# Graph attention and a routed expert layer on one core: order of the first projections, who scales the last chunk, and in which step a tile's residual, norm and routing are done

## The reference, cut to what matters

```python
def gnn(x, adj, W, b_W, a_vec, b_a):           # N = 2048 nodes, D = 128
    h = x @ W.T + b_W
    e = (h @ a1)[:, None] + (h @ a2)[None, :] + b_a[0]
    e = where(e > 0, e, 0.2 * e)
    scores = where(adj > 0, e, -9e15)
    return softmax(scores, axis=1) @ h

def ffn(x, Wr, br, W1, b1, W2, b2):            # 64 experts, 128 -> 256 -> 128
    logits = x @ Wr + br
    topk_logits, topk_idx = top_k(logits, 2)
    gates = softmax(topk_logits)
    # out = sum over the two chosen experts of gate * (relu(x W1 + b1) W2 + b2)

x = x + gnn(layernorm(x), adj, ...)
x = x + ffn(layernorm(x), ...)
```

## Time and profile before

| what | us |
|---|---|
| median of 3 runs (293.38 to 293.85) | 293.51 |
| the profiled execution's own time | 295.59 |
| its span, from the first to the last instruction | 293.8 |
| busy: PE, DVE, ACT, POOL | 229.1, 220.0, 173.5, 167.5 |
| mean granted TensorE clock, as a share of full speed | 0.895 |

### The profile page before, as it was taken

One profiled execution on the slowest core, in us unless ns is written; L12 is line 12 of the kernel. 1 busy time (PEld: TensorE's weight loads), 2 busy tenths in 40 slices (PEclk: granted clock), 3 DMA queues, 4 the chain that ended last, 5 costly groups with the idle time before them and its releaser, 6 DMA issues.

```text
span 293.8 us, 6191 instructions
## 1 busy us (share of the span) xinstructions
PE 229.1 (78%) x1849; PEld 219.6 (75%) x1849; DVE 220.0 (75%) x643; ACT 173.5 (59%) x386; POOL 167.5 (57%) x193
## 2 busy tenths in 40 slices
PE   1491698596959779586997463999999999999840
PEld 1271698596959769585996352999999999999840
DVE  4858959949599986999997550588888666666554
ACT  2754665755765496567653602688786777777410
POOL 5840104325175982978886565344688888876500
PEclk9998599988897979899799655799999999999995
DMA  6992730644847386150298012212226830100057
GB/s 165 223 190 48 101 62 1 122 130 134 224 74 186 120 214 182 45 232 31 64 425 331 32 48 59 72 58 74 66 81 220 275 138 31 38 27 31 26 186 254
DMA packets 11120, 36.88 MB, mean 126 GB/s; under 512 B 2257, under 2 KB 2833, under 8 KB 10321
## 3 DMA queue, kind: packets, MB, share of 16 engines
q0 software_dynamic: 5232, 14.98, 22.5%
q1 hardware_dynamic: 5424, 21.11, 21.1%
q10 hardware_dynamic: 432, 0.40, 0.6%
HBM read 39.36 MB, written 5.51 MB: 153 GB/s over the span
## 4 chain that ended last, share of the span: by engine, by line
PE 44%; DVE 28%; POOL 9%; DMA 7%; issue 6%; ACT 4%; SPq 1%; POOLq 0%; DVEq 0%; ACTq 0%
PE bank L1089 16%; PE bank L1101 15%; DVE arena L697 7%; PE bank L986 6%; DVE arena L691 6%; POOL rstd L403 3%; POOL table L420 3%; POOL nm L405 2%; DMA arena<-result 2%; DMA xs<-in_x 2%; DVE arena L682 2%; DVE xs L703 1%; PE bank L938 1%; PE bank L1078 1%; ACT rows_in L546 1%
## 5 line engine op out<-in xcount | busy, mean ns | idle before, releaser
L986 PE MATMUL bank<-arena 128*128 128x130 f32 x512 | 64.8, 287 | 3.0 <-ACT arena L540 3.0
L986 PEld LDWEIGHTS bank<-arena 128*128 128x128 f32 x512 | 63.5, 204 | 3.9 <-issue 3.9
L1089 PE MATMUL bank<-arena 128*128 x384 | 61.1, 284 | 0.1
L1101 PE MATMUL bank<-w2s,arena 128*128 x384 | 59.2, 277 | 0.2 <-issue 0.2
L972 PE MATMUL bank<-ident,arena 128*128 128x128 f32 x256 | 39.0, 317 | 22.4 <-DVE arena L697 22.3
L420 POOL DMA_INDIRECT table<-rows_in,pos x32 | 46.8, 1464 | 15.9 <-issue 7.8
L972 PEld LDWEIGHTS bank<-ident,arena 128*128 128x128 f32 x256 | 34.9, 165 | 24.0 <-DVE arena L697 24.0
L1089 PEld LDWEIGHTS bank<-arena 128*128 128x128 f32 x384 | 52.1, 197 | 0.6 <-issue 0.3
L1101 PEld LDWEIGHTS bank<-w2s,arena 128*128 128x128 f32 x384 | 51.1, 194 | 0.6 <-issue 0.6
L868 DVE SCALAR_TENSOR_TENSOR arena<-bank,arena 128x128 f32 x96 | 33.6, 350 | 22.5 <-PE bank L1101 15.2
L599 ACT ACTIVATE arena<-bank,arena 128x128 f32<-128x128 f32 x96 | 35.2, 366 | 19.3 <-PE bank L1089 14.4
(11 more groups left out here) (191 smaller groups left out, 270.9 us busy)
## 6 DMA issues: line engine op xcount, KB each, us to landing
arena<-in_adj POOLq DMA_DIRECT2D x16, 512.0 KB, 6.5
w2s<-in_w SPq DMA_DIRECT2D x8, 768.0 KB
arena<-in_w SPq DMA_DIRECT2D x6, 1024.0 KB
arena<-in_w SPq DMA_DIRECT2D x4, 512.0 KB
w2s<-in_w SPq DMA_DIRECT2D x4, 512.0 KB
xs<-in_x SPq DMA_DIRECT2D x4, 256.0 KB, 6.4
arena<-result SPq DMA_DIRECT2D x2, 512.0 KB, 4.3
arena<-result SPq DMA_DIRECT2D x4, 256.0 KB, 6.2
```

The lines of the kernel that those rows point to most:

```text
L986: ins = pe.matmul(OB[t % 2][:, 0:D + 2], pt_r[:, t % 2, j, :], h[:, j, :], start=(j == 0), stop=(j == T - 1))
L1089: ins = pe.matmul(hp(p, b), w1u[:, p % UW, P * b:P * b + P], xT_all[:, bass.ds(column, P)], start=True, stop=True)
L1101: ins = pe.matmul(yp(p), hT[:, p % UH, b, :], w2s[:, bass.ds(u, 1), b, :].rearrange("p e d -> p (e d)"), start=(b == 0), stop=(b == HB - 1))
```

## The change

It has eight edits.

1. TensorE's start: after the first two chunks' transposes come piece 0 of the score row, the transposes of chunk 2, piece 1, the projections of chunk 0, the transposes of chunk 3, pieces 2 and 3 back to back, and behind them the projections of chunks 1 to 3.
2. VectorE scales chunk 3 (with a semaphore of its own, `s_norm3`); ScalarE scales chunks 0 to 2 only. GpSimd issues the adjacency loads 2 and 3 behind the last `nm2`. VectorE does `penalty(0)` right after its first copy, and `scores(0)` after two of the eight `h_evac`; six follow it. `s8` is made in two pieces.
3. VectorE's loop: `residual(s-3)` stands ahead of `leaky(s-1)`, where `residual(s-2)` stood behind it; `residual(13)` follows the loop.
4. ScalarE's norms come in even steps from 4 on, ahead of evac: norm(s-4), norm(s-3). GpSimd's `rstd_of` follows, one step later and behind that step's load; tile 8's scatter goes from step 14 to 15.
5. Routing on TensorE and ScalarE stands inside a tile: `route_a(q)` at the head of attend(LAST[q]+2), `route_b(q)` in its middle; ScalarE's `route_a` in the middle of that tile's evac. Group 4 had this form before.
6. `top2` and `place`: two operations over k become one of twice the size (L733, L750); the position is written to its integer tile in one step.
7. The row numbers (`ids`) are written to `rows_out` once, by GpSimd at the start, no longer by VectorE in each `place` (L757).
8. The last sums with b2 go in four groups of four tiles, where there were six groups.

```diff
-    PLACED = [..., (1, 7, 14), (2, 8, 14), (2, 9, 15)]
+    PLACED = [..., (1, 7, 14), (2, 8, 15), (2, 9, 15)]
...
 # gpsimd
+            pool.tensor_copy(rows_out[:, :, :, ID_COL], ids[:, :, :])
...
-                if c < 3:
-                    load(c + 1)
+                if c == 0:
+                    load(1)
+            load(2)
+            load(3)
...
             for s in range(T):
-                if s >= 3 and s % 2 == 1:
-                    rstd_of(s // 2 - 1)
                 if s + 5 < T:
                     load(s + 5)
+                if s >= 4 and s % 2 == 0:
+                    rstd_of(s // 2 - 2)
...
 # scalar
-            scale(3)
...
             def evac(t):
                 for b in range(4):
+                    for q in range(NG):
+                        if b == 2 and t == LAST[q] + 2:
+                            route_a(q)
...
-                for q in range(INLOOP):
-                    if s == LAST[q] + 3:
-                        route_a(q)
+                if s >= 4 and s % 2 == 0:
+                    norm(s - 4)
+                    norm(s - 3)
                 if s >= 1:
                     evac(s - 1)
-                if s >= 3 and s % 2 == 1:
-                    norm(s - 3)
-                    norm(s - 2)
...
+            norm(T - 4)
+            norm(T - 3)
             evac(T - 1)
             norm(T - 2)
-            route_a(4)
             route_b(4)
...
 # vector
-                for k in range(TOPK):
-                    ins = dve.tensor_tensor(hot[:, k, kept(q), :], ..., ALU.is_equal)
-                link(ins)
+                link(dve.tensor_tensor(hot[:, :, kept(q), :], ..., ALU.is_equal))
...
-                link(dve.scalar_tensor_tensor(posf[:, :, 0:n], ...))
                 dve.wait_ge(s_gate, q + 1)
-                dve.tensor_copy(rows_out[:, rows, :, ID_COL], ids[:, rows, :])
                 dve.tensor_copy(rows_out[:, rows, :, GATE_COL], ...)
-                dve.tensor_copy(pos[:, rows, :]..., posf[:, :, 0:n]).then_inc(s_pos, 1)
+                dve.scalar_tensor_tensor(pos[:, rows, :]..., idxf..., float(STRIDE), rank...).then_inc(s_pos, 1)
...
             xT_evac(0)
-            xT_evac(1)
             penalty(0)
+            dve.wait_ge(s_nm, 4)
+            for t in range(12, T):
+                ins = dve.tensor_scalar(xh[:, t, :], xs[:, t, :], rstd[:, t:t + 1], nm2[:, t:t + 1], ALU.mult, ALU.add)
+            ins.then_inc(s_norm3, 1)
+            xT_evac(1)
             xT_evac(2)
+            penalty(1)
             dve.wait_ge(s_was, 1)
             h_evac(0)
             h_evac(1)
-            penalty(1)
-            for c in range(2, 6):
-                h_evac(c)
+            dve.wait_ge(s_hs, 2)
+            dve.tensor_scalar(s8[:, 0:4], h[:, 0:4, D], 1.0 - SLOPE, None, ALU.mult).then_inc(s_s8, 1)
             scores(0)
-            h_evac(6)
-            h_evac(7)
+            for c in range(2, 8):
+                h_evac(c)
...
+                if s >= 3:
+                    residual(s - 3)
                 leaky(s - 1)
-                if s >= 2:
-                    residual(s - 2)
...
+            residual(T - 3)
             leaky(T - 1)
             residual(T - 2)
...
 # tensor
             def attend(t):
                 if t >= 2:
                     pe.wait_ge(s_x1, t - 1)
-                if t == T - 1:
-                    route_a(4)
+                for q in range(NG):
+                    if t == LAST[q] + 2:
+                        route_a(q)
                 for j in range(T):
                     b = j // CB
-                    if t == T - 1 and j == T // 2:
-                        route_b(4)
+                    for q in range(NG):
+                        if j == T // 2 and t == LAST[q] + 2:
+                            route_b(q)
```

More of the change, by code:

```diff
@@ L451, in _ @@
             rstd_of(8)
-            for q in (4, 5):
+            for q in range(4, NG):
                 for t in range(START[q], START[q + 1]):
@@ L622, in _ @@
                     fetch(p + UW - 1)
-            for q in range(NG):
+            for q in range(4):
                 act.wait_ge(s_ct, q + 1)
-                act.activation(combT[:, START[q] * P:START[q + 1] * P], bank[q][:, 0:SIZE[q] * P], ACT.Copy).then_inc(s_cts, 1)
+                act.activation(combT[:, q * 512:q * 512 + 512], bank[q][:, :], ACT.Copy).then_inc(s_cts, 1)
         @block.vector
@@ L899, in _ @@
             dve.tensor_scalar(y_all[:, NB - 1, :], y_all[:, NB - 1, :], slot_gate[:, NB - 1:NB], None, ALU.mult).then_inc(e_last, 1)
-            for q in range(NG):
+            for q in range(4):
                 base(q)
-            dve.wait_ge(s_base, NG)
+            dve.wait_ge(s_base, 4)
             for c in range(2):
@@ L954, in _ @@
             pe.wait_ge(s_was, 1)
-            for b in range(4):
-                scores_row(b)
-                if b < 2:
-                    turn_x(b + 2)
-                if b < 3:
-                    project(b)
-            project(3)
+            scores_row(0)
+            turn_x(2)
+            scores_row(1)
+            project(0)
+            turn_x(3)
+            scores_row(2)
+            scores_row(3)
+            for b in range(1, 4):
+                project(b)
             def turn(t):
@@ L1027, in _ @@
                 attend(s)
-                for q in range(INLOOP):
-                    if s == LAST[q] + 1:
-                        route_a(q)
-                    if s == LAST[q] + 2:
-                        route_b(q)
+                for q in range(NG):
                     if s == LAST[q] + 3:
```

58 lines of the change are left out of this document (30 added, 28 removed).

## The result

| what | before | changed |
|---|---|---|
| median (lowest to highest) in us, 4 runs each | 293.49 (293.38 to 293.85) | 282.27 (281.66 to 282.31) |
| the profiled execution's own time | 295.59 | 282.29 |
| its span | 293.8 | 280.5 |
| busy: PE, DVE, ACT, POOL | 229.1, 220.0, 173.5, 167.5 | 223.1, 217.5, 170.6, 166.5 |
| mean granted clock | 0.895 | 0.914 |

The ratio is 0.9611, with a 95% interval of 0.9594 to 0.9628: 11.2 us faster, where the forecast said 9.3. The chain of work that ended last (page, part 4) answers to the earlier trace rows: TensorE's share went up, GpSimd's down from 9% to 5%, ScalarE's from 4% to 1%.

The account below looks back on a forecast made before the run. The prediction took the attention loop as VectorE's work plus waits, the expert part as TensorE's. Terms −0.2 − 13.2 + 0.5 + 3.8 − 1.3 + 1.1 = −9.3 us gave a 284.2 us median; 8-in-10 range 280.4 to 288.4.

Parts of the forecast that it names:

- top2's wait of about 3 us at tile 9: Predicted sign in the loop: VectorE's top2 waits about 3 us for the logits at tile 9.
- The start, −0.2: Before the loop: reordered start and moved scalings bring scores(1) to 26.5, −0.2 us, between −1.0 and +1.5.
- The lower bound of −1.0: Best case for the start: piece 1 of the score row runs at full clock, −1.0 us.
- The residual, −13.2 + 0.5: VectorE's loop: residual one step later removes 13.2 us of waits for attend; 0.5 us stays at tile 0.
- The norms and the routing, +3.8: Loop, even steps: norms ahead of evac make logits late where routing is due, costing 0.6 plus 3.2 us.
- Tile 5: Routing in the loop: logits ready at D + 9.0, top2 reached at D + 8.4, costing +0.6 us.
- D: The prediction's time origin: the start of leaky(s-1) in an even step, when the statistics are ready.
- Tile 9: Routing in the loop: GpSimd late to the power behind scatters and a load, logits at D + 11.5, +3.2 us.
- The rival that GpSimd starves: Loop: every pair's nm after D + 8, each of six even steps waits 3.3 us; 299.7 us, chance 0.06.
- place and top2, −1.3: VectorE's routing operations: place −0.25 us for each of three in the loop, merged pairs −0.55 us.
- After the loop, +1.1: Last leaky to gather: norms and two more scatters delay evac(15) and top2(4), place gains 0.3; +0 to +3 us.
- Against the median: Conversion of the total: profiled execution 2.1 us over the median, so 286.3 us becomes 284.2 us.

Follow-up runs that it names:

- 4: Changed kernel with the start of the kernel before (TensorE's start order, chunk 3's scaling and what goes with them undone): 281.75 us, ratio 0.9581 to the kernel before.
- 7: Changed kernel with the pair of norms in the middle of evac, behind its second block, instead of ahead of it: 282.97 us, ratio 0.9593.
- 8: Changed kernel with GpSimd's power for tiles 12 and 13 ahead of tile 9's scatters instead of behind: 282.06 us, ratio 0.9576.
- 9: Changed kernel run again with no edit, as yardstick, profiled a second time: 282.37 us, ratio 0.9612 to the kernel before.
- the second profile: Kernel before, run and profiled once more with no edit: 293.97 us, span 292.2 us.
- 2: Changed kernel with only the later residual undone, so residual(s-2) stands behind leaky(s-1) again: 300.39 us, ratio 1.0225 to the kernel before.
- 3: Kernel before with only the residual moved, residual(s-3) ahead of leaky(s-1); norms, power and routing left in place: 304.5 us, ratio 1.0365.
- 10: Changed kernel with five of VectorE's penalty operations (tiles 9, 10, 11, 13, 15) made by ScalarE: 281.58 us, ratio 0.959 to the kernel before.
- 12: Changed kernel with five penalties on ScalarE and tile 3's scatters moved from step 11 to 12, behind the power: 282.61 us, ratio 0.9589.
- 5: Changed kernel with the merged top2 and place operations apart again, position and id copies back on VectorE: 285.57 us, ratio 0.9683.
- 6: Changed kernel with route_b of the first four groups behind attend instead of in its middle: 288.01 us, ratio 0.9772 to the kernel before.

## Why the prediction was right, and where its sizes were off

Most of its signs came as written: no residual among the waits of the loop but 0.61 us at tile 0 (written: 0.5), norms that wait 1.6 to 4.4 us, scores(0) at 21.3 (21.0), scores(1) at 26.66 (26.5), and 114.3 us behind the gather. The one that did not is top2's wait of about 3 us at tile 9, which was 0.79; with it the last leaky came at 137.5 (140) and the gather at 166.2 (169).

- **The start, −0.2.** Measured −0.1 in this profile, and 4 found nothing in the times; the means of the profiles differ by −0.7. The lower bound of −1.0 was put on a fast piece 1, and experiments 7, 8 and 9 had one (1.02 us against 1.89 here); the granted clock reads 1.00 in all four, so it is not what tells them apart. The four scalings on VectorE took 1.0 us (13.49 to 14.52; I took 0.9).
- **The residual, −13.2 + 0.5.** Right: the waits of 13.2 (12.3 in the second profile) became 0.61. The sum's 0.6 for a penalty and 2.3 for a leaky are 0.60 and 2.26 from start to start in the kernel before (penalty at 43.44, leaky at 44.04, reciprocal at 46.30). That this step rests on the others, 2 and 3 showed; the prediction counted it as if it stood alone. Of the 22.2 us that residual waited in 2, 16.4 lie where GpSimd came late to the power, a case that this term does not have.
- **The norms and the routing, +3.8.** This is the term that was mis-sized: 1.6 us (0.79 twice). Tile 5 was put at 0.6, on logits at D + 9.0; they came at D + 9.2 (D = 60.07), from an attend at a granted clock of 1.00 (66.30 to 69.20). Tile 9 was put at 3.2 by the sentence "I put the power's start at D + 2.9". The timeline of the changed kernel at tile 9:

```profile
88.49 1.85 POOL L422 DMA_INDIRECT table<-rows_in,pos  x1 [0.30 <-issue]
...
91.30 2.35 DVE L699 SCALAR_TENSOR_TENSOR arena<-arena,tneg 128x2048 f32<-128x2048 f32 x1
91.49 2.74 POOL L405 TENSOR_TENSOR rstd<-ve,expo 128x2 f32<-128x2 f32 x1 [0.50 <-DVE ve L715]
...
95.94 1.09 ACT L550 ACTIVATE rows_in<-xs,nm,rstd 128x256 f32<-128x256 f32 x2 [3.29 <-POOL nm L407]
...
97.60 2.02 PE L995 MATMUL bank<-arena 128*128 128x130 f32 x16
...
100.50 0.43 DVE L720 TENSOR_TENSOR lg<-bank,bss 128x256 f32<-128x256 f32 x1 [0.79 <-PE bank L1011]
```

The power began at D + 0.2, after 0.50 us in which GpSimd stood idle: its scatters (0.98, 1.57 and 1.85 us for the last three) had ended in time. Half an attend took 2.02 us at a granted clock of 1.00, where I had counted on a slow one, and the logits were read at D + 9.2, as at tile 5, not at D + 11.5. In step 4 I had counted on 2.3 us in which TensorE stands, as in the earlier trace rows, and on a slow attend behind them. With the transposes from D + 3.1, which took 1.91 us, and evac from D + 5.64 it stood 1.33 us (at most 1.46 ahead of a tile with routing, at 97.13), and no run of the changed kernel shows the slow attend there: attend(3) ran at a granted clock of 1.00 and ended at D + 10.2. Nor does the idle time alone tell the clock in this kernel: after 2.41 us the transposes at 79.21 took 3.40 us (granted clock 0.56), after 2.48 us those at 110.53 took 1.97 (1.00). So GpSimd was in time at tile 9, and the tile cost 0.79, as tile 5 did. The rival that GpSimd starves, with every nm after D + 8, did not come true in this kernel; a piece of it did with the residual where it was (2), and as soon as VectorE was made faster still (10, 12).
- **place and top2, −1.3.** VectorE's work in the loop fell by 1.7 us against the kernel before, 1.1 of it by these edits (5); the other 0.6 no run assigns. In time they came to 2.1 us, with some 1.1 of uncertainty from the two intervals; that the part above 1.3 lies behind the loop, where their operations follow one another with nothing beside them, fits the profile of 5 and isn't shown.
- **After the loop, +1.1.** +0.65 to +0.7 in the first profiles, −0.1 to 0 against the changed kernel's second one, within the 0.7 by which that stretch varies: sign not shown.
- **Against the median.** The sum was made for the profiled execution, 2.1 us above the median; 1.1 of these lie behind the gather, where both kernels vary alike, so it was right to take the 2.1 off. The changed kernel's profiled execution lay at its median, so the terms below explain the 13.3 us between two profiles, 2.1 more than the 11.2 between the medians. That the forecast of 9.3 misses the medians by 1.9 and not by 2.8, the sum of what its terms were off, is luck of the two executions.

With what was measured in place of what was put, −0.1 − 13.2 + 0.6 + 1.6 − 1.7 + 0.7 = −12.1, and 1.1 from the stretch behind the gather make 13.2 of the 13.3 between the two spans.

## What to carry to other kernels

When an engine waits for the end of a chain, ask which of its own later operations could stand in that wait; and move the consumer together with the producers, since half of such a reordering can be worse than none (+7 and +11 us here for a pair worth −11). Once the waits are gone, price an edit by whose operation it is: 4.4 us more of waits on VectorE cost 4.6 (6), while 1.3 us less for TensorE in a step gave nothing (7). And work taken from the bounding engine pays only up to the next engine's due time: 3.0 us were taken off here and no gain was left, because GpSimd's power was due just behind. And where single executions of one kernel differ by 2 to 3 us, a term under 1 us needs several profiles.

## What the runs showed that I had not expected

- How long one of GpSimd's scatters takes differs in these profiles with what VectorE runs beside it; its loads show no such difference. Three rows of the changed kernel: a load, a scatter, and a scatter with VectorE in short operations:

```profile
85.70 0.61 POOL L371 DMA_DIRECT2D arena<-in_adj  x1
...
132.01 2.94 POOL L422 DMA_INDIRECT table<-rows_in,pos  x1 [0.31 <-issue]
...
136.52 0.96 POOL L422 DMA_INDIRECT table<-rows_in,pos  x1 [0.30 <-issue]
```

The first scatter began 0.2 us after a leaky (131.80 to 134.12) and ended behind it. The load began under a leaky too (84.98 to 87.30) and was done at 86.31. This holds throughout: between scores(1) and the last leaky of the fourteen profiles, 50 loads began under a leaky or a scores, took 0.53 to 0.62 us and ended ahead of it; 127 scatters began so, took 1.3 to 3.1 us, and each ended 0.83 to 0.98 us behind it, whether it had begun 0.04 or 1.86 us into it. 139 scatters that began beside shorter operations took 0.95 to 1.32 us. What in a scatter waits no run separates. GpSimd's busy time in the loop (65.5 us) is therefore no measure of its work.
- GpSimd's small computing operations ended behind VectorE's long ones too: 2.75 us for the power that takes 0.73 beside short ones. The prediction says of them that one that starts under a long operation waits for its end and then runs. From scores(1) to the end of the last leaky of the fourteen profiles, 70 powers began under a leaky or a scores, 0.14 to 2.09 us into it; they took 2.80 down to 0.83 us, and each ended 0.57 to 0.65 us behind it. 19 beside shorter operations took 0.71 to 0.74. Of nm, 40 began so, 0.19 to 0.75 us into it, took 2.20 down to 1.59 and ended 0.05 to 0.06 behind it; 46 beside shorter operations took 0.18 to 0.36. Two cases stand at the very edge, both in experiment 2: a power that began 0.02 us ahead of a scores (124.71) took 2.94 and ended 0.65 behind it, and an nm that began 0.03 us into a leaky (157.85) took 0.20, the one that went the other way. What in these operations waits no run separates. Since D is such a boundary, a pair of power and nm ended at D + 4.60 for tile 3 and for tile 9 alike (47.66 to 52.26, 91.30 to 95.90).
